# A transformer-style block with chunked linear attention: one power of -0.5 per step in place of three, and feed-forward rows normalized later in the step

## The reference

```
x = x + attention(layernorm(x))
x = x + feed_forward(layernorm(x))
layernorm(x) = (x - mean) / sqrt(var + 1e-5)            # per row of 512

attention: xx = previous row - row; four mixes x + xx*maa_k/v/r/g
           r, k, v = mix @ W.T;  g = silu(mix @ Wg.T)    # 32 heads of 16
           per chunk of 64 rows: y = ((r k) * w_mat) v + (r state) * wb
                                 state = ws * state + (k * wk) v
           yn = (y - mean) / sqrt(var + EPS), per row and head of 16
           out = (yn * gamma + beta) * g @ Wo.T
feed_forward: fp16(x) @ W0.T + b0, gelu, fp16, @ W1.T + b1
```

## Time and profile before

| | |
|---|---|
| median of 3 runs | 2166.96 us (2165.43 to 2167.08) |
| profiled execution: its own time, its span | 2165.32 us, 2163.5 us |
| PE busy | 2073.6 us (96%) |
| DVE busy | 1874.7 us (87%), 4336 instructions |
| ACT busy | 1169.2 us (54%) |
| POOL busy | 378.8 us (18%) |
| DMA queue of SP | 67.9% of 16 engines' time |
| mean granted clock of PE | 0.986 |

### The profile page before, as it was taken

One profiled execution on the slowest core, in us unless ns is written; L12 is line 12 of the kernel. 1 busy time (PEld: TensorE's weight loads), 2 busy tenths in 40 slices (PEclk: granted clock), 3 DMA queues, 4 the chain that ended last, 5 costly groups with the idle time before them and its releaser, 6 DMA issues.

```text
span 2163.5 us, 58680 instructions
## 1 busy us (share of the span) xinstructions
PE 2073.6 (96%) x24056; PEld 1485.2 (69%) x24056; DVE 1874.7 (87%) x4336; ACT 1169.2 (54%) x1940; POOL 378.8 (18%) x331
## 2 busy tenths in 40 slices
PE   5678999999999999999999999999999999999998
PEld 4456677777667777667777766777776677777665
DVE  6888998888899888889988888998888998888861
ACT  6555455565545565545556554555555455565442
POOL 1111112111111211211121111112111112111120
PEclk8889999999999999999999999999999999999999
DMA  6545667776666777666677766667776667777667
GB/s 206 185 145 158 207 200 224 223 228 201 201 204 206 226 229 220 192 201 208 216 228 223 227 183 210 198 218 229 223 224 186 210 201 222 226 225 206 200 214 238
DMA packets 342987, 452.72 MB, mean 209 GB/s; under 512 B 183872, under 2 KB 221248, under 8 KB 342720
## 3 DMA queue, kind: packets, MB, share of 16 engines
q1 hardware_dynamic: 341088, 448.76, 67.9%
q10 hardware_dynamic: 1632, 0.21, 0.1%
HBM read 316.24 MB, written 25.17 MB: 158 GB/s over the span
## 4 chain that ended last, share of the span: by engine, by line
PE 52%; DVE 31%; issue 5%; SPq 2%; ACT 2%; DMA 1%; DVEq 0%; ACTq 0%
PE F L917 13%; PE F L888 12%; PE sc L719 6%; PE YT L747 6%; DVE mixf L227 6%; DVE att L1114 5%; PE B L719 4%; DVE S L1137 4%; PE YT L719 3%; DVE att L1108 3%; DVE mix L287 3%; DVE kv L1123 2%; PE B L868 2%; DVE gT L1144 1%; DVE dx L218 1%
## 5 line engine op out<-in xcount | busy, mean ns | idle before, releaser
L888 PE MATMUL F<-xT,ring 128*128 128x256 f16 x4096 | 484.9, 273 | 9.2 <-ACT hT L1396 3.6
L917 PE MATMUL F<-ring,hT 128*128 128x512 f16 x2016 | 475.3, 379 | 1.4 <-ACT hT L1396 1.4
L888 PEld LDWEIGHTS F<-xT,ring 128*128 128x128 f16 x4096 | 396.2, 98 | 72.5 <-issue 7.4
L917 PEld LDWEIGHTS F<-ring,hT 128*128 128x128 f16 x2016 | 189.6, 98 | 200.6 <-ACT hT L1396 3.3
L283 ACT ACTIVATE mix<-mixf 128x1024 f16<-128x1024 f32 x128 | 135.2, 1056 | 326.9 <-DVE mixf L227 213.8
L1396 ACT ACTIVATE hT<-F,b,f_rho 128x256 f16<-128x256 f32 x512 | 260.5, 565 | 36.4 <-PE F L888 36.2
L227 DVE SCALAR_TENSOR_TENSOR mixf<-dx,maa,xnT 128x256 f32<-128x256 f32 x512 | 270.7, 556 | 0.4 <-PEq L492 0.3
L719 PE MATMUL B<-mix,WT 128*128 128x256 f16 x2304 | 269.6, 274 | 0.0
L1519 POOL TENSOR_TENSOR Shl<-S,Shl 128x512 f16<-128x512 f32 x128 | 153.8, 1202 | 657.2 <-ACT Shl L1363 657.2
L719 PEld LDWEIGHTS B<-mix,WT 128*128 128x128 f16 x2304 | 223.9, 98 | 36.1 <-issue 0.2
L1363 ACT ACTIVATE Shl<-S 128x512 f16<-128x512 f32 x128 | 80.2, 627 | 239.0 <-DVE S L1137 131.9
(11 more groups left out here) (175 smaller groups left out, 3037.5 us busy)
## 6 DMA issues: line engine op xcount, KB each, us to landing
ring<-w_dram SPq DMA_DIRECT2D x512, 512.0 KB, 4.6
kx<-kT SPq DMA_DIRECT2D x96, 256.0 KB, 2.5
rx<-rT SPq DMA_DIRECT2D x96, 256.0 KB, 4.4
xa<-in_L_attn_x SPq DMA_DIRECT2D x32, 512.0 KB, 7.4
vbd<-vN SPq DMA_DIRECT2D x256, 64.0 KB, 2.8
x<-in_L_attn_x SPq DMA_DIRECT2D x32, 512.0 KB, 5.4
out<-x SPq DMA_DIRECT2D x31, 512.0 KB, 3.9
ring<-in_L_ffn_W SPq DMA_DIRECT2D x10, 512.0 KB, 8.5
```

The source lines that it names most:

```text
L888: mm = eng.matmul(F[:, j % 2, i * BT:(i + 1) * BT], ring[:, use % RING, i, a * C + kk * P:a * C + (kk + 1) * P], xT[:, :, kk, :], start=(k ...
L917: mm = eng.matmul(F[:, t, :], hT[:, k, rows(t)], ring[:, use % RING, i, a * C:(a + 1) * C], start=(k == 0 and a == 0), stop=(k == NH - 1 a ...
```

## The change

It takes the three powers of a step together. The tiles of variances (`rs_a`, `rs_r`, `rs_t`) hold, side by side, 2 columns for the block ahead (ROWS), 64 for the heads of block n - 1 (HEADS) and 2 for the feed-forward rows of block n - 2 (LATER); `has(n)` says which of them a step has, and one chain of eleven runs over those. Means and variances of both layernorms lie in one tile `mv`, so that one instruction adds epsilon for both and one makes both row means. The feed-forward rows' power moves from the end of a step into the next step's chain; with it `act_fnorm` moves on ACT behind the third mix and the second K copy. `dve_take_y(n, 1)` moves ahead of `dve_residual(n - 1, 1)` and the statistics. The head's normalization of y stands behind the chain. PE's, SP's and POOL's lists are unchanged.

```diff
-    LN_STEPS = 2 * NT + 2 + RSQRT_STEPS
-    LN_PER, GN_PER = 2 + RSQRT_STEPS, 1 + RSQRT_STEPS
+    ROWS, HEADS, LATER = range(3)
+    EDGES = (0, NT, NT + NT * H, 2 * NT + NT * H)
...
+    def has(n):
+        first = ROWS if n + 1 < nb else HEADS if n <= nb else LATER
+        last = LATER if n >= 2 else HEADS if n >= 1 else ROWS
+        return first, last
+
+    def of_rows(first, last):
+        return slice(int(first > ROWS), 1 + int(last == LATER))
+
+    def dve_row_var(eng, n):
+        first, last = has(n)
+        if first == ROWS:
+            eng.wait_ge(s_bn, 2 * NT * (n + 2))
+        if last == LATER:
+            eng.wait_ge(s_fbn, 2 * NT * (n - 1))
+        at = of_rows(first, last)
+        eng.tensor_scalar(rs_a[:, :].rearrange("p (k c) -> p k c", k=2)[:, at, 0:NT], mv[:, at, :, 1], LN_EPS, None,
+                          ALU.add).then_inc(s_va, 1)
+
+    def dve_power_half(eng, n, k):
+        first, last = has(n)
+        if k == 0:
+            eng.wait_ge(s_va, n + 2)
+            if first <= HEADS <= last:
+                eng.wait_ge(s_gn, n)
+        at = slice(EDGES[first], EDGES[last + 1])
+        rsqrt_step(eng, k, s_rs, RSQRT_STEPS * (n + 1), rs_a[:, at], rs_r[:, at], rs_t[:, at])
+
+    def dve_row_mean(eng, n):
+        at = of_rows(*has(n))
+        eng.wait_ge(s_rs, RSQRT_STEPS * (n + 2))
+        eng.scalar_tensor_tensor(out=rs_n[:, at, :], in0=mv[:, at, :, 0], scalar=-1.0,
+                                 in1=rs_r[:, :].rearrange("p (k c) -> p k c", k=2)[:, at, 0:NT],
+                                 op0=ALU.mult, op1=ALU.mult).then_inc(s_mean, 1)
...
     def dve_step(eng, n):
         att_n, tail, ff, ahead, late = in_step(n)
+        early = n <= 2
+        mixes = [(m, g) for m in (2, 3) for g in range(G)] if att_n else []
+
+        def mixing(count):
+            for _ in range(min(count, len(mixes))):
+                dve_mix(eng, n, *mixes.pop(0))
+
+        if n <= nb + 1:
+            if early:
+                mixing(G)
+            if ahead:
+                dve_stats(eng, n + 1, 0)
+            mixing(1)
+            if tail:
+                dve_variance(eng, n - 1, 1)
+            if ahead:
+                dve_stats(eng, n + 1, 1)
+            if att_n and early:
+                dve_K_lo(eng, n, 0)
+            if ahead:
+                for t in range(NT):
+                    dve_mean_var(eng, n + 1, t)
+            mixing(1)
+            if tail:
+                dve_head_var(eng, n - 1)
+            dve_row_var(eng, n)
+            if att_n and early:
+                mix_lo(eng, n, 2)
+            mixing(1)
+            for k in range(RSQRT_STEPS):
+                dve_power_half(eng, n, k)
+                if att_n:
+                    if k == 1 and not early:
+                        dve_K_lo(eng, n, 0)
+                    elif k == 6:
+                        dve_K_lo(eng, n, 1)
+                    elif k == 8 and not early:
+                        mix_lo(eng, n, 2)
+                    else:
+                        mixing(1)
+            dve_row_mean(eng, n)
+            if tail:
+                for t in range(NT):
+                    dve_normalized(eng, n - 1, t)
         if n > nb:
             dve_e(eng, n - 3)
...
             dve_state(eng, n, 3)
+            dve_take_y(eng, n, 1)
         if tail:
             dve_residual(eng, n - 1, 1)
-            dve_fln(eng, n - 1)
-        if att_n:
-            dve_take_y(eng, n, 1)
+            dve_f_stats(eng, n - 1)
...
     def act_fnorm(eng, f):
-        eng.wait_ge(s_fln, LN_PER * (f + 1))
+        eng.wait_ge(s_mean, f + 4)
...
-        if ff:
-            act_fnorm(eng, n - 2)
         if att_n:
             act_mix_hi(eng, n, 2)
             act_K_hi(eng, n, 1)
+        if ff:
+            act_fnorm(eng, n - 2)
```

More of the change, by code:

```diff
@@ L137, in program @@
     bn = sb("bn", [P, NT, 6])
-    mv = sb("mv", [P, NT, 2])
-    ln_a, ln_r, ln_t, ln_n = (sb(f"ln_{c}", [P, NT]) for c in "artn")
+    mv = sb("mv", [P, 2, NT, 2])
+    rs_a, rs_r, rs_t = (sb(f"rs_{c}", [P, 2 * (NT + NT * H)]) for c in "art")
+    rs_n = sb("rs_n", [P, 2, NT])
     xnT = sb("xnT", [P, G, BT + 1])
@@ L166, in program @@
     s_e0, s_n, s_x, s_t = (sem(f"s_{v}") for v in ("e0", "n", "x", "t"))
-    s_bn, s_ln, s_xn, s_X, s_xT, s_carry, s_dx, s_mix, s_mh, s_ml = (
-        sem(f"s_{v}") for v in ("bn", "ln", "xn", "X", "xT", "carry", "dx", "mix", "mh", "ml"))
+    s_bn, s_va, s_rs, s_mean, s_xn, s_X, s_xT, s_carry, s_dx, s_mix, s_mh, s_ml = (
+        sem(f"s_{v}") for v in ("bn", "va", "rs", "mean", "xn", "X", "xT", "carry", "dx", "mix", "mh", "ml"))
     s_xw, s_xwT = sem("s_xw"), sem("s_xwT")
@@ new lines, in program, with dve_stats, dve_mean_var @@
+    s_fbn, s_xh, s_fx, s_up, s_h, s_dn, s_e, s_o = (
+        sem(f"s_{v}") for v in ("fbn", "xh", "fx", "up", "h", "dn", "e", "o"))
+    ROWS, HEADS, LATER = range(3)
+    EDGES = (0, NT, NT + NT * H, 2 * NT + NT * H)
+    def dve_stats(eng, n, t):
+        if t == 0:
+            eng.wait_ge(s_xa, 16 * (n + 1))
+        eng.bn_stats(bn[:, t, :], xa[:, t, :]).then_inc(s_bn, 1)
+    def dve_mean_var(eng, n, t):
+        eng.wait_ge(s_bn, 2 * NT * n + t + 1)
+        eng.bn_aggr(mv[:, 0, t, :], bn[:, t, :]).then_inc(s_bn, 1)
@@ L576, in _ @@
             def _(eng):
[L577 to L580, removed]
+                for t in range(NT):
+                    dve_stats(eng, 0, t)
+                dve_ep(eng)
+                for t in range(NT):
+                    dve_mean_var(eng, 0, t)
+                dve_row_var(eng, -1)
+                for k in range(RSQRT_STEPS):
+                    dve_power_half(eng, -1, k)
+                dve_row_mean(eng, -1)
                 eng.memset(xnT[:, :, 0:1], 0.0).then_inc(s_carry, 1)
@@ L622, in program @@
     y = sb("y", [P, NT, C])
-    gn_s, gn_a, gn_r, gn_t = (sb(f"gn_{c}", [P, NT, H]) for c in "sart")
+    gn_s = sb("gn_s", [P, NT, H])
     ygT = sb("ygT", [P, G, BT])
@@ L1171, in dve_fln @@
             eng.wait_ge(s_fbn, 2 * NT * f + t + 1)
[L1172 to L1181, removed]
+            eng.bn_aggr(mv[:, 1, t, :], f_bn[:, t, :]).then_inc(s_fbn, 1)
     def dve_e(eng, f):
@@ L1199, in dve_step @@
         if n > nb:
             dve_e(eng, n - 3)
[L1201 to L1223, removed]
@@ L1224, in dve_step @@
         if att_n:
-            if not early:
-                mix_lo(eng, n, 2)
             dve_R_lo(eng, n, 0)
```

73 lines of the change are left out of this document (23 added, 50 removed).

## The result

| | before | after |
|---|---|---|
| median of the timed runs, us | 2167.02 (2165.43 to 2168.71, 4 runs) | 2205.7 (2204.59 to 2209.68, 4 runs) |
| ratio, 95% interval | | 1.0182 [1.0164, 1.0199] |
| profiled execution: time, span | 2165.32, 2163.5 | 2205.75, 2204.0 |
| DVE busy, instructions | 1874.7 us, 4336 | 1806.2 us, 3607 |

The change takes 729 of 4336 instructions off DVE and makes the kernel 38.7 us slower; 2204 was predicted. Lines of the new kernel that stand in for old ones: L918 for L888, L828 for L798, L871 for L841, L1132 for L1108, L1138 for L1114, L1554 for L1519, L1149 for L1125, L302 for L275, L254 for L227, L291 for L264, L1619 for L1584.

What follows compares the result with a forecast made beforehand. PE, then DVE, bound each step in a loop, with PE idle 0.2 of 63.30 us. 28 x 1.2 = 34, tail 3, head 0: 37 us on 2165.32 gives 2202, median 2204 us (+1.7%); 8-in-10 range 2167 to 2230.

Steps and rivals of the forecast that it cites:

- P and D: Each step: PE alone (P, 1066.30 to 1100.83), then DVE from first `dve_weigh` (D, 28.5 us); removed operations save nothing in P.
- The chain's end and xT: Merged DVE chain ends at 1082.2; SP issues xT<-xh at 1083.8 instead of 1079.15, 1.8 us to spare for `pe_up(0)`.
- rival 4: On DVE, 68-wide operations cost more than 0.26 us (say 0.35): +28, 2232 us; chance 0.10 together with rival 3.
- rival 3: xT lands over 6 us after issue, so PE's `pe_up(0)` waits: +28, 2232 us; chance 0.10 together with rival 4.
- The queue: On SP, everything from kx to mixf<-dx moves 1.4 us later, at most 2.3 to 2.6; 2.0 taken for mixf<-dx landing.
- The join's price: `act_x_join` on ACT starts 0.8 us after D begins, the free border being 0.5 before: 1.2 us taken per step.
- The weights: Weights behind vbd, 1.4 to 2 us later, idle PE 1 to 1.5 beside D, adding nothing while the join is later.
- granted clock unchanged: Sign in a steady period: the granted clock, 1.00 before, stays as it was.
- Where PE idles: Sign: PE's idle time before `pe_att_v(1)` grows from 0.2 to 1.4 us, with some before L888 for weights.
- DVE busy per period: Sign: DVE busy near 53 us where it was 57.15; 24 operations fewer at 0.16, 3.8 us per step.
- The tail: Step after the last attention block: weights behind xT on SP go out at 2094.3 instead of 2091.03, +3.3 us.
- The head: Steps 1 and 2: 2.5 us off before step 2 and `pe_up(0)` waiting for rows cancel to within 1 us; 0 taken.

Runs made afterwards that it cites:

- e1: Changed kernel with kx issued ahead of xT<-xh on SP instead of behind it: 2168.99 us, ratio 1.0006 to the kernel before.
- e9: Changed kernel with mixf<-dx issued on SP ahead of the weight load in front of it (use+4): 2181.0 us, ratio 1.0050 to the kernel before.
- e6: Changed kernel with the weight load behind vbd and out (use+5) issued ahead of them, right behind mixf<-dx: 2196.41 us, ratio 1.0132 to the kernel before.
- e10: Changed kernel with SP issuing mixf<-dx, then weight loads use+4 and use+5, then vbd: 2171.43 us, ratio 1.0013 to the kernel before.
- e3_before_late_xT: Kernel before, with one wait added on SP: xT<-xh not issued until the second half of kT is ready: 2194.87 us, ratio 1.0124.
- e12: Changed kernel with 44 unused matmuls filling PE's gap in the last step with a Wo: 2208.41 us, ratio 1.0180 to the kernel before.

## Why the prediction was right

- *P and D, and nothing to win in P*: right. e1 has 24 operations less per step and P and D of before, to 0.1.
- *The chain's end and xT*: predicted 4.65 later, measured 4.6. The operations 68 wide follow each other at 0.26 (1104.25, 1104.51), as taken; rival 4 falls. `pe_up(0)` waits in no steady step; rival 3 falls.
- *The queue*: kx 1.4 later as predicted; mixf<-dx 1.9 later at its issue and 1.75 at the join, for which I took 2.0, between 1.4 and 2.6.
- *The join's price*: D 29.46 on average, within the 29.3 to 30.3 given, but 0.86 more than before, where I took 1.2. It starts 0.4 us after D on average, not 0.8. This term of the sum was too large, 24 us (28 x 0.86) for 34. The experiments measured 24.7 (after less e9) and 25.0 (e6 less e10). The mechanism was right in kind, POOL's later work on DVE, but not in place: the two mixes take 2.02 beside POOL instead of 2.29, and `dve_weights_lo(1)` 2.24 instead of 1.28. So most of the price comes as one step of about 0.7 and not one for one; the wait of `dve_dx` adds 0.25 per step.
- *The weights*: here a step failed. "It runs beside D, which has 0.4 to 0.6 in hand against it, so it adds nothing while the join is the later one." The waits came (0.94 per step), but they add 0.28 per step, 8 us, which shows in P and not in D, because in 11 steps PE was the later one. Of these 8 us, 3.3 are the clock's: "granted clock unchanged" does not hold for two of the 28 periods. The runs put it at 9.3 (after less e6) or 9.6 (e9 less e10). This and the join's error nearly cancel: 1.14 measured for 1.2.
- *Where PE idles*: wrong in the same way. I expected it before `pe_att_v(1)`, from 0.2 to 1.4 per step; those waits hardly changed, 10.6 us before and 9.8 after. It stands at L918, earlier in the same stage, and where e6 takes it away there, some of it comes back before L828 and L871 (9.8 and 4.4 in the kernel after):

```profile
PE YT L828 <- DVE att L1138: 15.0, 30, 4.3
PE YT L871 <- issue: 10.3, 16, 1.4
PE F L918 <- DMA ring<-w_dram: 4.7, 2, 4.4
```

- *DVE busy per period*: predicted near 53, measured 55.32, and 54.44 in e1, where nothing is late. The 0.16 holds only for what stood in one piece: in the period of the earlier trace rows the 13 operations of the feed-forward chain cover 2.1 us that nothing else covers. The 13 of the chain for the block ahead, which stood between others, cover 0.3 alone. So the 24 gave back 2.7, and not 3.8. The other 0.9 are almost all in the eight operations of `dve_weights_lo`, 6.81 us in this period against 5.85 in e1. No term of the sum rests on it.
- *The tail*: 3.3 predicted, 6.2 measured. xT goes out 4.0 later there (101.6 us after the last `dve_dx` instead of 97.6), 1.7 more is the clock's, which the sum did not have, and 0.4 is left over. The head was put at nothing and measured 2.5; 1.1 of it is there in e1 too. I did not take it further.

The sum was 37 us and the spans differ by 40.5: 34 for 31.9 in the steady part, 3 for 8.7 at the ends. That the median lay 1.7 us from the forecast owes something to luck.

The Trainium skill (DMA: Bandwidth & Descriptors, Queues, rings and completion order) says that what one engine issues goes through one ring on each of the 16 DMA engines, consumed in ring order. The rows agree in so far as kx and all behind the late xT go out later too, by 1.4 to 1.9 us here and by 1.3 to 1.5 in e3_before_late_xT. Whether SP's issuing or the rings hold them, no run here separates.

## What to carry to other kernels

Before you make a product later, look at what stands behind its transfer in the same queue, not only at who reads it. Here xT had 1.8 us to spare for its own reader and cost 32 us through the loads behind it; changing places with one transfer gave it back. And before you count operations off an engine, look at the idle time of the engine that sets the period in that stage: 0.2 us was about all there was, whatever left DVE.

## What was not expected of the hardware

- In the last steps the granted clock fell to 0.50 in a gap of 5.2 us without a matmul and cost 1.7 us on the next 16 (3.69 us against 2.01 with the gap filled). By the Trainium skill (TensorE: Matmul & The Clock Gate, Part 1) the low state is the default and activity releases it; the filled gap agrees.
- Shorter waits did the same in the middle of dense work. In the steady parts of the kernel after, e9 and e12 the clock fell six times, behind waits of 1.95 to 3.08 us, each time at a price of 1.5 to 1.7 us; waits of 2.07 (e3), 2.09 and 2.36 (e12) brought no fall. So a wait for weights of some 2 us can cost nearly twice its length, and whether it does is not settled by its length.
- `dve_weights_lo(1)` takes 1.28 or 2.24 us and nothing between, by whether a POOL operation is still running when it starts; in the kernel before that operation ended 0.2 us ahead of it in 28 of 29 steps.
- Small DVE operations that wait for each other take 0.19 to 0.26 us from start to start. Removed, they gave back 0.16 of busy time each where they stood in one piece and far less where others stood between them.
